# Loads of sums two groups behind loads of rows, and GpSimd's work of the first phase in another order

## What is computed

```python
# attention over the 16 heads of one token (not over tokens): q, k, v are 16 x 16 per token
q, k, v = ln(x) @ Wq.T, ctx @ Wk.T, ctx @ Wv.T
x = x + softmax(einsum('bnhd,bngd->bnhg', q, k) * 0.25) @ v ... @ Wp.T + bp
y = ln(x)
shared = (silu(y @ sfc1.T) * (y @ sfc2.T)) @ sfc3.T
top_w, top_idx = top_k(y @ gate_w.T, 2); top_w = softmax(top_w)
moe = sum over the 2 chosen experts e of  w_e * silu(y @ w1[e].T) @ w2[e].T
out = x + moe + shared
```

## Time and profile before

| | |
|---|---|
| median of 3 runs | 1864.77 us (1860.51 to 1875.49) |
| profiled execution, its own time | 1852.7 us |
| its span | 1850.9 us |
| busy over the span: PE, DVE, POOL, ACT | 81%, 73%, 67%, 39% |
| first phase, 110 to 1160 us: PE, DVE, POOL busy of 1050.00 | 983.89, 914.51, 819.32; TensorE clock 1.00 |
| same stretch, transfers | DMA share 0.85, 184 GB/s |
| expert phase, 1300 to 1560 us: PE, DVE, POOL busy of 260.00 | 178.62, 136.03, 133.20; TensorE clock 0.85 |
| same stretch, transfers | DMA share 0.66, 196 GB/s |

### The profile page before, as it was taken

How to read it: one execution, slowest core, us unless ns; L and a number is a source line. 1 busy time by engine, 2 the same in 40 slices (tenths; PEclk the granted TensorE clock), 3 DMA queues, 4 the chain that set the end, 5 groups by cost and what they waited for, 6 DMA issues and landing times.

```text
span 1850.9 us, 50328 instructions
## 1 busy us (share of the span) xinstructions
PE 1504.5 (81%) x17109; PEld 1318.8 (71%) x17110; DVE 1345.4 (73%) x3378; ACT 726.3 (39%) x1346; POOL 1234.2 (67%) x1109
## 2 busy tenths in 40 slices
PE   5599999999999999999999999875667676666674
PEld 4588787877787878777878788764656665566563
DVE  6588888888888888888888888863445455454453
ACT  3344444454444444544454445331222222222231
POOL 4387777777777777778777877765455554454455
PEclk9799999999999999999999999987788888888887
DMA  8788889878887988789878887747666675666573
GB/s 208 166 186 180 179 201 182 180 169 213 176 177 160 227 176 174 161 221 183 173 173 216 174 175 157 191 176 237 193 208 199 189 209 161 194 203 198 179 209 115
DMA packets 945833, 344.74 MB, mean 186 GB/s; under 512 B 824088, under 2 KB 898730, under 8 KB 940288
## 3 DMA queue, kind: packets, MB, share of 16 engines
q1 hardware_dynamic: 901680, 216.53, 56.9%
q0 software_dynamic: 33600, 92.91, 14.2%
q10 hardware_dynamic: 10512, 34.79, 5.8%
HBM read 200.37 MB, written 148.15 MB: 188 GB/s over the span
## 4 chain that ended last, share of the span: by engine, by line
PE 40%; DVE 18%; issue 16%; SPq 11%; POOL 5%; DMA 5%; ACT 4%; another core or an unknown queue 1%; DVEq 0%; POOLq 0%; ACTq 0%
SPq L337 4%; SPq L331 4%; PE bank_y L1145 3%; ACT xn L613 3%; PE bank_a L1158 3%; PE bank_y L1143 3%; PE bank_y L1144 3%; PE bank_a L1143 3%; DVE ln_stats L897 2%; PE bank_z L1143 2%; DVE ctx_lo L880 2%; PE bank_a L1297 2%; PE bank_a L1145 2%; PE bank_a L1144 2%; PE bank_u L1143 2%
## 5 line engine op out<-in xcount | busy, mean ns | idle before, releaser
L400 POOL DMA_INDIRECT slots<-xn,slot_i x256 | 281.6, 1100 | 96.0 <-issue 55.7
L517 POOL DMA_INDIRECT sums<-v_area,tail x144 | 144.0, 1000 | 144.4 <-DVE v_area L1096 98.8
L517 POOL DMA_INDIRECT out<-v_area,tail x144 | 143.6, 997 | 135.6 <-DVE v_area L1096 91.6
L1386 PE MATMUL bank_a<-ident,k_area 128*128 128x128 f32 x576 | 96.1, 321 | 140.8 <-DMA k_area<-slots 140.3
L1386 PEld LDWEIGHTS bank_a<-ident,k_area 128*128 128x128 f32 x576 | 77.8, 165 | 150.7 <-DMA k_area<-slots 150.1
L1096 DVE SCALAR_TENSOR_TENSOR v_area<-bank_y,tail,v_area 128x256 f32<-128x256 f32 x288 | 121.4, 478 | 68.4 <-remote 31.2
L690 ACT ACTIVATE th<-bank_z 128x512 f32<-128x512 f32 x72 | 43.0, 597 | 280.9 <-remote 135.6
L1075 DVE TENSOR_TENSOR xn_lo<-v_area,xn_hi 128x512 fp32r<-128x512 f32 x72 | 50.2, 698 | 140.2 <-ACT xn_hi L697 71.4
L409 POOL DMA_INDIRECT sums<-v_area,slot_i x128 | 128.1, 1001 | 33.2 <-issue 29.4
L1143 PE MATMUL bank_y<-wsh_out_hi,hid_hi 128*128 128x256 f32 x512 | 143.1, 279 | 1.3 <-POOL hid_lo L431 1.3
L1144 PE MATMUL bank_y<-wsh_out_lo,hid_hi 128*128 128x256 f32 x512 | 142.8, 279 | 0.0
(11 more groups left out here) (222 smaller groups left out, 5283.9 us busy)
## 6 DMA issues: line engine op xcount, KB each, us to landing
k_area<-slots SPq DMA_DIRECT2D x288, 129.0 KB
v_area<-sums SPq DMA_DIRECT2D x288, 128.0 KB
kv_dram<-w_sb SPq DMA_DIRECT2D x32, 1024.0 KB
x_sb<-in_x_in SPq DMA_DIRECT2D x32, 512.0 KB
ctx_sb<-in_ctx_t SPq DMA_DIRECT2D x32, 512.0 KB
q_dram<-q_sb SPq DMA_DIRECT2D x32, 512.0 KB
k_area<-kv_dram SPq DMA_DIRECT2D x256, 64.0 KB
w_sb<-q_dram SPq DMA_DIRECT2D x256, 64.0 KB
```

Source lines behind the costliest of these rows:

```text
L400: pool.indirect_dma_start(slots[j], bass.IndirectOffsetOnAxis(ap=slot_i[:, par, j, i:i + 1], axis=0), row_of[j][:, i, :], None).then_inc(S ...
L517: pool.indirect_dma_start(target, bass.IndirectOffsetOnAxis(ap=tail[:, r, t, 1 - j:2 - j].bitcast(u32), axis=0), y_ring[:, r, t, :], None, ...
L1386: last = nc.tensor.transpose(A[t // 2][:, t % 2 * C + k * P:t % 2 * C + (k + 1) * P], x_ring[:, r, t, CHANNEL[j] + k * P:CHANNEL[j] + (k + ...
```

## The change

Two parts, and one small one on ScalarE. (1) In the expert phase SP issues the loads of sums of group n-2 behind the loads of rows of group n (`LAG = 2`), so the wait for `added` is one for the group six before. Row numbers are read anew for the sums (two table reads per group for one). At the seam between the two lists, the sums of the last two groups of the first list are loaded behind the rows of the third and fourth group of the second. (2) On GpSimd, `ln1_power` goes from behind `ln2_power` to behind `xn2_split`, one scatter of sums goes behind `scale_probs`, and the scatters of rows stand 5, 2 and 1 around the `hid_split` steps 0 and 1, 2, and 3 (before 4, 1, 1 and 2, each followed by one step). (3) On ScalarE the rounding of x of chunk c+2 goes ahead of the two copies of the turned rows, behind a wait for TensorE's down product (`acc_full`).

```diff
--- before.py
+++ after.py
@@ -315,56 +315,64 @@
             for j in range(TOP):
                 sp.dma_start(slots[j][NO_TILE:NO_TILE + P, :], pad[:, 0, :]).then_inc(S["no_tile_stored"], 16)
                 sp.dma_start(sums[j][NO_TILE:NO_TILE + P, :], pad[:, 0, 0:C]).then_inc(S["no_tile_stored"], 16)
-            row_regs = [[sp.alloc_register(f"tile_row{r}_{t}") for t in range(4)] for r in range(4)]
-
-            def tile_rows(n, r):
-                sp.reg_load(row_regs[r], slot_row[0:1, bass.ds(n * 4, 4)])
-                return [sp.snap(reg, min_val=0, max_val=NO_TILE) for reg in row_regs[r]]
-
-            def load_x(j, n, r, at_rows, first):
+            x_regs = [sp.alloc_register(f"x_row{t}") for t in range(4)]
+            sums_regs = [sp.alloc_register(f"sums_row{t}") for t in range(4)]
+
+            def tile_rows(regs, n):
+                sp.reg_load(regs, slot_row[0:1, bass.ds(n * 4, 4)])
+                return [sp.snap(reg, min_val=0, max_val=NO_TILE) for reg in regs]
+
+            def load_x(j, n, r, first):
+                rows = tile_rows(x_regs, n)
                 if not first:
 
 
                     sp.wait_ge(S["tail_ready"], at(1, n - 4, 1))
                     sp.sem_inc(S["slot_free"], 1)
                 for t in range(4):
-                    sp.dma_start(x_ring[:, r, t, :], slots[j][bass.ds(at_rows[t], P), :]).then_inc(S[f"loaded{r}"], 16)
-
-            def load_sums(j, n, r, at_rows, first):
+                    sp.dma_start(x_ring[:, r, t, :], slots[j][bass.ds(rows[t], P), :]).then_inc(S[f"loaded{r}"], 16)
+
+            def load_sums(j, n, r, first):
+                rows = tile_rows(sums_regs, n)
                 if not first:
                     sp.wait_ge(S[f"added{r}"], at(16, n - r, 0))
                 for t in range(4):
-                    sp.dma_start(y_ring[:, r, t, :], sums[j][bass.ds(at_rows[t], P), :]).then_inc(S[f"held{r}"], 16)
+                    sp.dma_start(y_ring[:, r, t, :], sums[j][bass.ds(rows[t], P), :]).then_inc(S[f"held{r}"], 16)
+
+            LAG = 2
+
+            def load_steps(j, n, new):
+                for r in range(4):
+                    load_x(j, n + r, r, False)
+                    load_sums(j, n + r - LAG, (r - LAG) % 4, new and r < LAG)
 
             sp.wait_ge(S["rows_ready"], 1)
             sp.wait_ge(S["no_tile_stored"], 2 * 16 * TOP)
             sp.wait_ge(S["padded1"], 2 * 16 * 3)
             sp.wait_ge(S["scattered1"], 16 * BPC * CHUNKS)
-            first_rows = [tile_rows(q, q) for q in range(4)]
-            for q in range(4):
-                load_x(FIRST, q, q, first_rows[q], True)
+            for r in range(4):
+                load_x(FIRST, r, r, True)
             sp.wait_ge(S["based"], 16 * BPC * CHUNKS)
             sp.wait_ge(S["padded0"], 2 * 16 * 3)
-            for q in range(4):
-                load_sums(FIRST, q, q, first_rows[q], True)
-            with sp.Fori(4, QUADS - 3, 4) as q:
-                for r in range(4):
-                    at_rows = tile_rows(q + r, r)
-                    load_x(FIRST, q + r, r, at_rows, False)
-                    load_sums(FIRST, q + r, r, at_rows, False)
+            for r in range(4 - LAG):
+                load_sums(FIRST, r, r, True)
+            load_steps(FIRST, 4, True)
+            with sp.Fori(8, QUADS - 3, 4) as q:
+                load_steps(FIRST, q, False)
             sp.wait_ge(S["scattered0"], 16 * BPC * CHUNKS)
-            second_rows = [tile_rows(QUADS + r, r) for r in range(4)]
             for r in range(4):
-                load_x(SECOND, QUADS + r, r, second_rows[r], False)
+                load_x(SECOND, QUADS + r, r, False)
+                if r >= 4 - LAG:
+                    load_sums(FIRST, QUADS + r - 4, r, False)
             for r in range(4):
                 sp.wait_ge(S[f"added{r}"], 16 * QUADS)
-            for r in range(4):
-                load_sums(SECOND, QUADS + r, r, second_rows[r], True)
-            with sp.Fori(QUADS + 4, TOP * QUADS - 3, 4) as q:
-                for r in range(4):
-                    at_rows = tile_rows(q + r, r)
-                    load_x(SECOND, q + r, r, at_rows, False)
-                    load_sums(SECOND, q + r, r, at_rows, False)
+            for r in range(4 - LAG):
+                load_sums(SECOND, QUADS + r, r, True)
+            load_steps(SECOND, QUADS + 4, True)
+            with sp.Fori(QUADS + 8, TOP * QUADS - 3, 4) as q:
+                load_steps(SECOND, q, False)
+            for r in range(4 - LAG, 4):
+                load_sums(SECOND, TOP * QUADS + r - 4, r, False)
 
 
         @block.gpsimd
@@ -449,28 +457,26 @@
             ln1_power(1, False)
             scale_probs(0)
             ln2_power(0)
-            ln1_power(2, False)
             ctx_split(2)
             x_split(2)
 
-            def body(c, par, first, ahead_2):
+            def body(c, par, first, ahead_2, last=False):
                 xn2_split(c - 1)
+                if not last:
+                    ln1_power(c + 1, False)
                 if not first:
-                    scatter_base(c - 2, par, range(3))
+                    scatter_base(c - 2, par, range(2))
                 scale_probs(c)
                 if not first:
-                    scatter_base(c - 2, par, range(3, BPC))
-                scatter(c - 1, 1 - par, SCATTERS[:4])
-                hid_split(c - 1, range(1))
-                scatter(c - 1, 1 - par, SCATTERS[4:5])
-                hid_split(c - 1, range(1, 2))
-                scatter(c - 1, 1 - par, SCATTERS[5:6])
+                    scatter_base(c - 2, par, range(2, BPC))
+                scatter(c - 1, 1 - par, SCATTERS[:5])
+                hid_split(c - 1, range(2))
+                scatter(c - 1, 1 - par, SCATTERS[5:7])
                 hid_split(c - 1, range(2, 3))
-                scatter(c - 1, 1 - par, SCATTERS[6:])
+                scatter(c - 1, 1 - par, SCATTERS[7:])
                 hid_split(c - 1, range(3, SB))
                 ln2_power(c)
                 if ahead_2:
-                    ln1_power(c + 2, False)
                     ctx_split(c + 2)
                     x_split(c + 2)
 
@@ -479,7 +485,7 @@
                 body(c, 0, False, True)
                 body(c + 1, 1, False, True)
             body(CHUNKS - 2, 0, False, False)
-            body(CHUNKS - 1, 1, False, False)
+            body(CHUNKS - 1, 1, False, False, True)
 
             def pads(j):
 
@@ -613,12 +619,14 @@
                     st = nc.scalar.activation(xn2[:, i, XN2], h2[:, par, i, :], ACT.Identity, bias=ln2_shift[:, i:i + 1], scale=ln2_rstd[:, i:i + 1])
                 st.then_inc(S["xn2_ready"], 1)
 
-            def turned_out(c, ahead_2):
+            def turned_out(c, ahead_2, start=False):
+                if ahead_2:
+                    if not start:
+                        act.wait_ge(S["acc_full"], at(2, c, 0))
+                    x_round(c + 2)
                 for k in range(KT):
                     act.wait_ge(S["t2_full"], at(KT, c, k + 1))
                     nc.scalar.activation(xn2_t[:, k, :], XN2T_BANKS[k][:, :], ACT.Copy).then_inc(S["t2_out"], 1)
-                if ahead_2:
-                    x_round(c + 2)
                 for k in range(KT):
                     act.wait_ge(S["t2_out"], at(KT, c, k + 1))
                     st = nc.scalar.activation(xn2_hi[:, k, :], xn2_t[:, k, :], ACT.Copy)
@@ -646,7 +654,7 @@
             o_round(0)
             ctx_round(2, 0)
             ln2(0, 0, True)
-            turned_out(0, True)
+            turned_out(0, True, True)
 
             def body(c, par, first, ahead, ahead_2):
                 exps(c, range(2))
```

## The result

The kernel after takes 1932.0 us in the median (1921.7 to 1948.9, 4 runs) against 1862.6 for the kernel before: ratio 1.038, 95% interval 1.028 to 1.048, slower. Timed again beside the kernel before, it gave 1.046 (1.038 to 1.054). The forecast was 1811 and faster. The ratios of this document leave out single runs over 1.5% above the fastest of their kernel: one of the kernel before, one of `sums22_only` and one of `p1_split_first`.

What follows compares the result with a forecast made beforehand. TensorE's waits were taken to limit the first phase's gain, the SP queue to bound the expert phase. 33 + 10 + 11 = 54 us off the 1864.8 median gave about 1811; own range 1785 to 1830, 8 in 10 within 1766 to 1850.

Steps and rivals of the forecast that it cites:

- the race: First phase: whether VectorE's `bias_add` or GpSimd's hidden split takes the SBUF port first; 1.57 us a chunk gained or 0.5.
- The cap of 2.06 us a chunk: First phase: TensorE's three waits per chunk, 1.06, 0.51 and 0.49 us; no edit can bring more, about 62 us.
- (b): First phase: `bias_add` and the scatters of rows come earlier, so TensorE waits less for `o_split`; ends 0.5 and 1.57 us a chunk.
- The term of 33 us: First-phase gain forecast: 1.1 us a chunk times 30.
- two splits in a row: First phase: two adjacent hidden splits hold `bias_add`, leaving `o_split` where it is, 0 to 0.3 us a chunk; about 1838, chance 0.17.
- (c): Expert phase, SP queue: rows no longer wait behind landed sums; about 0.17 us a group times 60 groups, 10 us gained.
- (d): Start of the expert phase: eight loads of sums instead of sixteen stand ahead of group 4's rows; 11 us gained, bounds 7 and 13.
- (e): Seam between the two lists: later sums of groups 34 and 35 set against fewer loads ahead; 0, bounds +10 and -5.
- Slower: Expert phase: loads of sums always among GpSimd's scatters, +1.4 us a group over 64 groups; about 1911, chance 0.08.

Runs made afterwards that it cites:

- sums22_only: Kernel before with only two scatters of sums ahead of `scale_probs` and two behind it (before 3 and 1): 1913.4 us, 1.028.
- p1_split_first: Kernel before with the GpSimd and ScalarE changes, no SP part, each two scatters of rows put behind a hidden split: 2042.5 us, 1.098.
- act_only: Kernel before with ScalarE's edit alone (x rounded ahead of the copies of the turned rows): 1833.1 us, 0.990.
- order_only: Kernel before with only GpSimd's new order of five scatters of rows, then hidden splits 0 and 1 in a row: 1918.6 us, 1.031.
- sp_only: Kernel before with the change to the SP queue alone: 1861.4 us, 1.000.
- after_old_order: Kernel after with GpSimd's scatters of rows and hidden splits back in the order of before: 1921.2 us, 1.030.
- ln1_only: Kernel before with only `ln1_power` moved behind `xn2_split`: 1868.6 us, 1.008.
- sums22_pause2: Kernel before with two sums scatters each side of `scale_probs`, plus a short GpSimd instruction before the row scatters, its tile behind all others: 1872.1 us, 1.008.
- act_sp: Kernel before with ScalarE's edit and the SP part: 1694.4 us, 0.938, in the chip 3 series; 1823.3, 0.983, when repeated.
- act_exp_pause: Kernel before with ScalarE's edit and a short GpSimd instruction amid each expert group's scatters, its four numbers ahead of other tiles: 1876.7 us, 1.039.

## Why the prediction was wrong

**Right.** `gap` takes 297 ns in the median (2001 in the earlier trace rows; 0.3 us of holding forecast), `hot_sum` 675 ns where the earlier trace rows had 1.60 us, and the wait of TensorE ahead of the z product is gone. `bias_add` takes 1.22 to 1.77 us, between the two ends of the race. ScalarE's edit is worth the 1% (chunks of 36.0 us in `act_only`). SP's wait for landed sums is gone but for one at the seam. The cap of 2.06 us a chunk was right for a gain and said nothing of a loss.

**The step that failed** is in (b): "TensorE, 0.5 us earlier, asks at 692.7: its wait of 1.06 becomes 0 to 0.4". It took z and u for as prompt as before and moved only what stands behind them. I had seen that "the first scatter of rows can go 1.4 us earlier, at 680.1" and counted it as a gain for the splits. It closed the break of 1.28 us between the scatter of sums and those of rows, while the 2 and 2 put one scatter more in front; the run of 5 with a break became one of 7. The wait became 3.3 us, and the clock, for which the sum had no term, took 1.25 on top. The term of 33 us was -90.5. The cost of making a VectorE wait go away was that what the wait had kept apart met.

**The rival "two splits in a row"** was right in its mechanism: in `order_only` `bias_add` waits out both splits. It was to end "1.0 us later than one split would make it", and with the 1.5 us by which the change was to bring it forward "just where it is now", at no cost. `order_only` doesn't have these 1.5 us, and there it takes 2.1 us longer than before (4.03 for 1.89) and costs 3.1%. So by my estimate the rival was 0.6 us short (2.1 - 1.5), and it too had no term for the clock. In after it doesn't occur, since the late signals pull the two splits apart.

**Expert phase, (c) to (e).** The forecast was a gain of 21 us; measured are 14.6 and, in the second pair of profiles, 25.3 (596.6 and 605.9 in before, 582.0 and 580.6 in after). That this fits is luck, since the parts don't. For **(c)** the groups are to be measured by ScalarE's tanh, from group 4 to 35 and from 40 to 71: 7.6 and 7.7 us in before (7.7 and 7.9 in the second profile), 7.4 and 7.2 in after (7.3 and 7.2), 7.6 and 7.4 in `sp_only`, where 0.17 a group less was forecast. That the SP queue "is itself the bound" was half of it: in `sp_only` TensorE's wait for rows fell from 70.6 to 38.9 of 260 us, and the groups got hardly shorter. **(d)** The rows of group 4 do go out 5 to 6 us earlier (7.5 forecast), but the first addition of group 4 comes only 1 to 2 us earlier (60.9 and 61.7 us behind the first load of rows in place of 62.0 and 64.0), in place of 11. **(e)** The seam costs about 6 us where I set 0: from the tanh of group 35 to that of group 40 it is 47.2 and 47.8 us in before, 52.9 and 53.8 in after and 52.5 in `sp_only`.

Nor is the gain clearly the SP part's. The expert phase takes 596.8 us in `sp_only` and 606.6 in `after_old_order`, which have the part, and between 583.4 (`ln1_only`) and 605.9 in the kernels that have it as before. One profile of each can't settle what the part gives while signals are late.

The rival "Slower" named 1911, near the result, by a mechanism that isn't the one: the loads of the SP queue are no slower in after than in before (four loads of rows span 2.1 and 2.2 us, in before 2.3 and 2.2).

What stays open: why a run of scatters keeps TensorE's signals. The experiments show that it does, not how. Nor is it known why three begun scatters are enough in the expert phase and not in the first, or what the 0.8% is that `sums22_pause2` still costs.

## What to carry to other kernels

A wait that an edit removes may have been what kept two streams apart: before counting it as gain, write down what will now run in an unbroken row on the other engine. On a program with one core, a wait "by remote", or a tanh that starts microseconds behind the product it reads, is a row to follow before any sum is made; here ScalarE spent 136 us of the kernel before in it, and breaking the runs was worth 26 us, and 47 beside the SP part, more than any edit of the change. Change one thing at a time, and put new tiles behind all others.

## What the runs showed of the hardware

- Three or four indirect scatters in a row on GpSimd kept TensorE's signals back, in the median by 3 to 5 us in the first phase and 6 in the expert phase, and let them go together some 1.4 us behind the last; TensorE's next products ran on. One instruction of 1.0 us in the run prevented most of it. The Trainium skill has TensorE push its signal once PSUM has acknowledged the writes (Perfetto Trace Analysis, Tensor Engine Instruction) and has TensorE and ScalarE never wait for anyone at SBUF's ports (SBUF — State Buffer, Who interferes with whom). The trace agrees for TensorE's matmuls, which ran on from 732.84; of signals that rule says nothing, and the one of this product came at 737.28. Whether its acknowledgement or its way was late, no trace here shows.
- In one series none of this happened, with the same programs: before took 1808 in place of 1857, and `act_sp` 1694 in place of 1823. It was the only series on chip 3.
- A VectorE instruction with two inputs in SBUF that started 0.64 us ahead of two GpSimd splits was held by both: 4.03 us in the median, where beside one split it took 1.89. So it was with `hot_sum` before, which started 0.47 us ahead of `scale_probs` and ended 0.05 us behind it.
- Moving the tiles of the first phase by 16 bytes cost 2.7 us a chunk (`act_exp_pause` against `act_sp`), with the DMA share at 1.00 in place of 0.89.
- An idle time of 3.87 us of TensorE is followed by a granted clock of 0.50 (1.2 GHz), and its matmuls of 256 columns then start 0.21 us apart in place of 0.113.
